# Keeping a bf16 copy of w1 in HBM, written in the first FFN group and reloaded in the other three

## The reference

```python
x = x + attn(_layernorm(x), W_qkv, W_out)
# feed-forward on x of (B, 2048, 1024): w1 (1024, 4096), w2 (4096, 1024)
h = jax.nn.relu(jnp.einsum('bsd,dw->bsw', _layernorm(x), w1) + b1)
x = x + jnp.einsum('bsw,wd->bsd', h, w2) + b2
```

## Time and profile before

| | |
|---|---|
| median of two timed runs | 1320.85 us (1314.60 and 1327.09) |
| the profiled execution, its device time | 1318.62 us |
| its span on the slowest core, core 7 | 1317.1 us |
| spans of the eight cores | 1291.5 to 1317.1 us |
| TensorE busy, core 7 | 989.3 us (75%) |
| VectorE, ScalarE, GpSimd busy | 472.9, 411.4, 101.2 us |
| read from HBM, written to it | 159.54 MB, 8.39 MB |

### The profile page before, as it was taken

The page is one execution under the profiler, slowest core; times in us unless marked ns, Lnnn a source line. Parts: engine busy times, 40 slices in busy tenths (PEclk is TensorE's granted clock), DMA queues, the critical chain, the costliest instruction groups (busy, mean ns, idle before and its releaser), DMA issues.

```text
span 1317.1 us, 12722 instructions; the slowest of 8 cores (1291.5 to 1317.1 us)
## 1 busy us (share of the span) xinstructions
PE 989.3 (75%) x4656; PEld 393.4 (30%) x4656; DVE 472.9 (36%) x638; ACT 411.4 (31%) x443; POOL 101.2 (8%) x131
## 2 busy tenths in 40 slices
PE   0189688585858586776946287997699887987897
PEld 0045222131213132222311133443244333443343
DVE  0451332636354544536351632313240324122301
ACT  0044076574757566564758100001000100010000
POOL 2200200000000000000000001110102001200110
PEclk9999878696979788897968588999999888998899
DMA  9900711010000002000200069896779768988876
GB/s 245 137 4 1 72 16 10 1 17 0 9 9 0 1 0 33 0 1 1 33 0 1 0 93 126 130 163 128 109 130 152 157 93 131 151 166 127 126 119 141
DMA packets 94332, 93.19 MB, mean 71 GB/s; under 512 B 40000, under 2 KB 72768, under 8 KB 94272
## 3 DMA queue, kind: packets, MB, share of 16 engines
q0 software_dynamic: 85248, 75.57, 41.2%
q1 hardware_dynamic: 9024, 16.80, 4.1%
HBM read 159.54 MB, written 8.39 MB: 127 GB/s over the span
## 4 chain that ended last, share of the span: by engine, by line
PE 63%; DVE 14%; DMA 13%; issue 4%; ACT 3%; DVEq 2%; ACTq 0%; POOL 0%; POOLq 0%
PE arena L720 17%; PE arena L675 13%; PE arena L508 11%; DMA wstage<-w 10%; PE arena L365 9%; PE arena L453 6%; DVE tmp_sb L603 5%; PE arena L287 4%; DVE oscr_sb L525 3%; DVE x_sb L614 3%; DMA wstage<-wout 2%; DVEq L51 2%; PE arena L468 2%; PE arena L239 1%; DMA x_sb<-x 1%
## 5 line engine op out<-in xcount | busy, mean ns | idle before, releaser
L481 ACT ACTIVATE p_sb<-arena,cst_sb 128x1024 bf16<-128x1024 f32 (+1 forms) x320 | 290.9, 986 | 100.3 <-PE arena L453 61.4
L508 PE MATMUL arena<-p_sb,vaug_h 128*128 128x512 bf16 (+3 forms) x640 | 192.2, 386 | 144.7 <-DVE oscr_sb L525 94.3
L675 PE MATMUL arena<-lnf_sb,wstage 128*128 128x512 bf16 x1024 | 250.1, 410 | 60.4 <-DMA wstage<-w 54.6
L720 PE MATMUL arena<-w2stage,h_sb 128*128 128x512 bf16 x1024 | 221.7, 379 | 4.0 <-DVE h_sb L688 4.0
L688 DVE TENSOR_SCALAR h_sb<-arena,b1c_sb 128x512 bf16<-128x512 f32 x128 | 96.1, 751 | 224.1 <-PE arena L675 224.1
L675 PEld LDWEIGHTS arena<-lnf_sb,wstage 128*128 128x128 bf16 x1024 | 105.4, 104 | 204.0 <-issue 102.4
L720 PEld LDWEIGHTS arena<-w2stage,h_sb 128*128 128x128 bf16 x1024 | 99.9, 98 | 125.8 <-issue 5.9
L365 PE MATMUL arena<-lnf_sb,wstage 128*128 128x512 bf16 x512 | 125.6, 402 | 8.3 <-DMA wstage<-wqkv 8.3
L453 PE MATMUL arena<-qpair,kpair 64*128 64x512 bf16 (+3 forms) x640 | 125.1, 387 | 4.9 <-DVE kpair L388 4.9
L508 PEld LDWEIGHTS arena<-p_sb,vaug_h 128*128 128x128 bf16 x640 | 42.7, 100 | 207.3 <-issue 206.0
L381 DVE CAST qpair<-arena 64x512 bf16<-64x512 f32 x64 | 43.7, 683 | 150.1 <-PE arena L365 149.5
(11 more groups left out here) (37 smaller groups left out, 495.1 us busy)
## 6 DMA issues: line engine op xcount, KB each, us to landing
wstage<-w POOLq DMA_DIRECT2D x32, 1024.0 KB, 11.1
w2stage<-w POOLq DMA_DIRECT2D x64, 512.0 KB, 6.9
x_sb<-x SPq DMA_DIRECT2D x4, 2048.0 KB, 25.7
y<-y_sb SPq DMA_DIRECT2D x16, 512.0 KB, 5.1
wstage<-wqkv POOLq DMA_DIRECT2D x24, 256.0 KB, 12.7
wstage<-wout POOLq DMA_DIRECT2D x4, 512.0 KB, 21.1
b1c_sb<-b SPq DMA_DIRECT2D x32, 0.5 KB, 7.2
identb_sb<-identf POOLq DMA_DIRECT2D x1, 32.0 KB, 8.6
```

The source lines that it names most:

```text
L481: e.activation(AP(p_sb, (si_ % 3) * 1024, [[3 * 1024, 128], [512, 2], [1, w_]]), AP(arena, b_ + off_, [[AR, 128], [512, 2], [1, w_]]), AF. ...
L508: e.matmul(AP(arena, (4 + hx) * 512 + off_, [[AR, 128], [1, w_]]), vaug_h[:, hx, j_ * 128:(j_ + 1) * 128], AP(p_sb, (si_ % 3) * 1024 + hx ...
L675: (lambda s_, dc_, fb_, wp_: lambda e: e.matmul(bankap(fb_, TF), AP(wstage, s_ * 1024 + dc_ * 512 + wp_ * 128, [[8 * 1024, 128], [1, 128]] ...
L720: (lambda s_, ww_, c2_, dh_, t_: lambda e: e.matmul(bankap(t_, 512), h1_sb[:, ww_, 128 * c2_:128 * (c2_ + 1)], w2stage[:, s_, 512 * dh_:51 ...
```

## The change

A DRAM tensor w1b of 1024 x 4096 bf16 is added (8 MB for each core). In group 0 the quads of w1 are loaded and cast by POOL as before, and ScalarE also stores each quad from wstage to w1b. The slots of such a quad are free when its last matmul and its store are both done. In groups 1 to 3 the quads are loaded from w1b in bf16, by DMAs that ScalarE issues. w2 is loaded as before. The other edits let `slot_free` hold a list, and add the new semaphores to the final wait.

```diff
+    w1b_d = nc.dram_tensor("w1b", [D, W1N], BF16, kind="Internal")
...
-        def load_slot_quad(in_ap, out_dims):
+        def _slot_waits(s, n):
+            w = []
+            for i in range(n):
+                v = slot_free[s + i]
+                w.extend(v if isinstance(v, list) else [v])
+            return w
+
+        def load_slot_quad(in_ap, out_dims, eng="gpsimd", pre="dw"):
...
-            w = [slot_free[s + i] for i in range(4)]
-            cnt = add("gpsimd",
+            cnt = add(eng,
                       (lambda oa, ia: lambda e: e.dma_start(oa, ia))(out_ap, in_ap),
-                      waits=w, inc=f"dw{s}", amt=16)
-            return s, (f"dw{s}", cnt)
+                      waits=_slot_waits(s, 4), inc=f"{pre}{s}", amt=16)
+            return s, (f"{pre}{s}", cnt)
...
                 if ww % 4 == 0:
-                    sp, dwp = load_slot_quad(
-                        AP(w1_d, 128 * ww,
-                           [[W1N, 128], [128 * W1N, DC], [1, 512]]),
-                        [[512, DC], [1, 512]])
+                    w1ap = [[W1N, 128], [128 * W1N, DC], [1, 512]]
+                    if g == 0:
+                        sp, dwp = load_slot_quad(
+                            AP(w1_d, 128 * ww, w1ap),
+                            [[512, DC], [1, 512]])
+                        dsb_c = add("scalar",
+                                    (lambda s_, ww_, a_: lambda e:
+                                     e.dma_start(
+                                         AP(w1b_d, 128 * ww_, a_),
+                                         AP(wstage, s_ * 1024,
+                                            [[8 * 1024, 128], [512, DC],
+                                             [1, 512]])))(sp, ww, w1ap),
+                                    waits=[dwp],
+                                    inc=f"dsb{(ww // 4) % 2}", amt=16)
+                        wb_pend = (f"dsb{(ww // 4) % 2}", dsb_c)
+                    else:
+                        sp, dwp = load_slot_quad(
+                            AP(w1b_d, 128 * ww, w1ap),
+                            [[512, DC], [1, 512]],
+                            eng="scalar", pre="dh")
+                        wb_pend = None
...
                     for i in range(4):
-                        slot_free[s + i] = ("mm", mm_f1)
+                        slot_free[s + i] = ([("mm", mm_f1), wb_pend]
+                                            if wb_pend else ("mm", mm_f1))
```

More of the change, by code:

```diff
@@ L40, in build_program @@
     y_d = nc.dram_tensor("y", [S, D], F32, kind="ExternalOutput")
+    w1b_d = nc.dram_tensor("w1b", [D, W1N], BF16, kind="Internal")
     seq = []
-    C = {"dx": 0, "dwb": 0, "dbc": 0, "dy0": 0, "dy1": 0, "dy2": 0, "dy3": 0,
+    C = {"dx": 0, "dwb": 0, "dbc": 0, "dsb0": 0, "dsb1": 0,
[1 row of a table added]
          "dq0": 0, "dq1": 0, "dq2": 0, "dq3": 0,
@@ L48, in build_program @@
         C[f"dw{_i}"] = 0
+        C[f"dh{_i}"] = 0
     def vdrain():
@@ L132, in load_slot @@
                       (lambda oa, ia: lambda e: e.dma_start(oa, ia))(out_ap, in_ap),
-                      waits=[slot_free[s]], inc=f"dw{s}", amt=16)
+                      waits=_slot_waits(s, 1), inc=f"dw{s}", amt=16)
             return s, (f"dw{s}", cnt)
-        def load_slot_quad(in_ap, out_dims):
+        def _slot_waits(s, n):
[5 more added lines that the diff above has]
+        def load_slot_quad(in_ap, out_dims, eng="gpsimd", pre="dw"):
             while slot_ctr[0] % 4:
@@ L153, in load_slot_pair @@
             out_ap = AP(wstage, s * 1024, [[8 * 1024, 128]] + out_dims)
-            w = [slot_free[s], slot_free[s + 1]]
+            w = _slot_waits(s, 2)
             cnt = add("gpsimd",
@@ L776, in build_program @@
                 f1_bank_free[b] = out_bank_free[b]
-        add("sync", None, waits=[("dx", C["dx"]), ("dbc", C["dbc"])] +
+        add("sync", None, waits=[("dx", C["dx"]), ("dbc", C["dbc"]),
+                                 ("dsb0", C["dsb0"]), ("dsb1", C["dsb1"])] +
                           [(f"dy{i}", C[f"dy{i}"]) for i in range(4)] +
-                          [(f"dq{i}", C[f"dq{i}"]) for i in range(4)])
+                          [(f"dq{i}", C[f"dq{i}"]) for i in range(4)] +
+                          [(f"dh{i}", C[f"dh{i}"]) for i in range(8)])
         add("gpsimd", None,
```

## The result

The changed kernel took 1302.61 us in the median of 11 runs, the kernel before 1319.61 us in 10. The ratio is 0.988, with an interval of 0.985 to 0.991: 16 us or 1.2% faster. A second measurement, beside the last experiment, gave 0.986 (0.981 to 0.990). The forecast was 1294.3 us, 1.8% faster.

What follows compares the result with a forecast made beforehand. The prediction took w1 loading to bound the first half of each feed-forward group. From 1318.6 us it took 32.3 for groups 1 to 3 and added 8 for group 0's stores, giving 1294.3 us, range 1272 to 1322.

Steps and rivals of the forecast that it cites:

- The bound and its threshold: w1 half of each group: w1 loading limits; a load landing within 6.98 us of issue is hidden, above that excess is paid.
- The cost of a bf16 load: Groups 1 to 3: 4.1 us of engine work, 1.5 fixed and 0.9 of issuing, so landing in 6.5 us.
- the line through the two casting loads: DMA packet cost from casting w1 and w2 loads: 47 ns per KB read over 17 ns, so 64 ns per 1 KB.
- The exposed first load: Start of groups 1 to 3: the first load, behind ScalarE's copies, loses its cover and is exposed for 6.5 us.
- The stores in group 0: Group 0's w1 half: eight 1 MB stores, 3.5 us of work each, lose 8 us, between 0 and 28.
- the hold, my second way to the same sum: Group 0: a slot waits for its store before reloading; its chain takes 22 to 23 us per pair of quads.
- The row of the mixed window: Trace window where y stores and w1 loads together filled a DMA share of 0.90; taken to mean stores aren't free.
- The w2 halves: Second half of each group: stays at 55.41 us, with moved traffic counted at nothing.
- The first (1273 us): Rival for the whole kernel: loads land in about 4 us, stores run beside loads; 1273 us, chance 0.20.
- The second: Rival in groups 1 to 3: loads land in 7.8 us, a wait replaces the one removed; 1316 us, chance 0.16.
- The third: Rival for loads and stores: a packet of 1 KB written costs 111 ns whatever is read; 1373 us, chance 0.10.
- the 2% line: Whole kernel: a measurement can tell about 2% (26 us) from no change, a line at 1294.4 us.

Runs made afterwards that it cites:

- the last experiment: precopy_w2 and, beside it on the same chip, the changed kernel measured again; ratios to the kernel before 0.942 and 0.986.
- bf16_pool: The changed kernel, but POOL issues the bf16 loads of groups 1 to 3, where it issued the casting ones; ratio to the kernel before 0.966.
- y_late: The changed kernel, but SyncE sends the y stores of groups 0 to 2 behind the next group's first two loads; ratio 0.977, 1290.15 us.
- stores_only: The changed kernel, but groups 1 to 3 load float32 w1 by casting POOL loads as before, so w1b is written and never read; ratio 1.009.
- stores_no_hold: stores_only, but stores of the same shape come from lnf_sb and the slots don't wait for them; ratio 1.004.
- early: The changed kernel, but ScalarE issues the first two quads of groups 1 to 3 ahead of its four copies; ratio 0.968, 1283.39 us.
- split_queues: The changed kernel, but in groups 1 to 3 POOL issues the first two bf16 quads and ScalarE the other six; ratio 0.966.
- precopy_w2: precopy_paced, but group 0's first four w2 loads wait for attention's last instruction, not the first quad's matmuls; ratio 0.942, 1250.35 us.
- precopy_paced: split_queues without quad stores; POOL's HBM-to-HBM casting copies write w1b in attention, each held until TensorE reaches its head pair; ratio 0.952, 1257.30 us.

## Why the prediction was right or wrong

**The bound and its threshold: right.** The w1 half waited for its loads. Once a load landed inside a quad's 6.98 us, the waits inside a group went, and with them the matmuls at 1.2 GHz behind them: 256 matmuls in 57 to 58 us in place of 64 in 14 to 17.

**The cost of a bf16 load: right to 0.6 us, with its fixed part split wrongly.** A stretch of group 1 in the changed kernel, 935 to 975 us, gives it:

```profile
q10 hardware_dynamic: 5709, 5.75, 50.5%
...
wstage<-w1b ACTq DMA_DIRECT2D x5, 1024.0 KB, 6.0
```

50.5% of 40 us over 5709 packets are 57 ns each, 3.6 us a load; the line through the two casting loads gave 64 ns and 4.1 us. (On cores 1 and 7 the same stretch gives 51 ns.) The landing of 5.9 us was forecast as 6.5, so 2.3 us are left beside the work, where the sum had 1.5 fixed and 0.9 of issuing. The total is right and the split isn't: I had allowed 2.4 us for ScalarE to issue a load of 1024 rows, and an issue holds its queue for 0.37 us. The Trainium skill ("DMA: Bandwidth & Descriptors", section "Anatomy of one DMA") has, for a DMA on the software queue, about 2 us plus the bytes at 436 GB/s, an estimate of 4.4 us here. This case's loads are slower on either queue, 5.9 us on ScalarE's and 6.7 on POOL's in bf16_pool, and the rate is part of it: 1.05 MB in 3.4 to 3.6 us is 290 to 310 GB/s.

**The exposed first load: right in kind, 4 us too small in each group.** The step that failed is the sentence that the y stores and the early w2 loads "are nearly through by then". The first load was costed as if alone, 6.5 us after the last copy. It waited 12.0 us on the mean after the last transpose, 10.7 after the copy. The w2 loads were nearly through indeed: on core 0, whose first load left at 910.51 us, 0.05 MB of them moved between 910 and 925 us, though POOL sent the last at 903.58. The y stores weren't: 1.90 of their 2.10 MB moved in that stretch. They leave 2 to 6 us before the load and are 5.2 us of work (1.3 us each). y_late takes them away and finds 7.3 us, or 6.0 after the copy, about the forecast size. I counted a transfer that had been issued as one that was done.

The groups' account closes in the table's measure. The first waits cost 3 x 4.2 = 12.6 us more than forecast. The 3 us a group for a slow start and late loads were 1.2 too many, 3.6 in all. And the forecast started from core 7, whose groups 1 to 3 are 4.5 us longer in sum than the mean core's. Together that is 13.5 us, close to the 12.9 between the 32.3 us forecast for these groups and the 19.4 of the table.

**The stores in group 0: right.** 8 us were forecast for group 0, 8.9 came, and stores_only alone gave 8.3. A store is 3.2 us of work where I took 3.5. Traffic is most of it by the profile of stores_no_hold; the hold, my second way to the same sum, is the smaller part there, and the measured times leave its size open. The row of the mixed window spoke rightly for a price.

**The w2 halves: right for the change,** 55.41 us. early shows how little was needed to lose that.

**The rivals.** The first (1273 us) needed a load in 4 us; it took 5.9. The second had the right kind of event, a wait in the place of the one removed, at another place: not in each pair, but once at a group's start. The third, one price for a packet of any size, is refuted by 57 ns against 111 ns.

The time lay inside the range, and the gain is clear of noise but below the 2% line, on which the forecast sat. Some luck is in the time: the groups gained 13 us less than forecast, and part of that came back because the slowest core drew nearer to the others, which the sum didn't have. Of the wait at each group's start, the place in ScalarE's list is the cause (early and bf16_pool both remove it), and the y stores are somewhat under half of its size (4.7 of 10.7 us).

## What to carry to other kernels

When a load moves to another engine's queue, look at what stands ahead of it there and what it was prefetched behind before: here 24 loads landed in about half the time, and more than half of the gain (70.7 us a group in place of the 60 to 61 of early and bf16_pool, from 77.2) was lost on the three that lost their prefetch. A queue of its own is good for the load that is needed next, and bad for one that is needed later: such a load belongs behind the urgent ones on the same queue. Data that is only cast and reused can be cast while the DMA engines idle, in another phase of the kernel; that was worth more than the change itself (from 0.966 in split_queues to 0.942 in precopy_w2).

## What the runs showed of the hardware that was not expected

- An issue of a load of 1024 rows held ScalarE's queue for 0.37 us, less than the 0.98 us of a y store of 128 rows on SyncE, so the number of rows alone doesn't set the time of an issue. The two are on different engines, and no run issues one DMA from both. The view of the line that issues the loads in the changed kernel gives the smallest, the median and the largest duration in ns:

```profile
L153 ACTq DMA_DIRECT2D wstage<-w1b x24: 366/366/788, 910.5 to 1231.6; - x24
```

- Two queues share the engines even when one has far more time: in early, w1b loads took 25 us to land, and w2 loads 13.8. The Trainium skill ("DMA: Bandwidth & Descriptors", section "Queues, rings and completion order") says each engine goes round robin between the queue rows with work, by packets; the 846 and 1079 packets of the two queues in that stretch agree in kind, where the shares are 71.7% and 30.1%.
- A copy from HBM to HBM with a cast, eight times 1 MB written, ran beside attention without changing its length in precopy_paced and precopy_w2 (starts of 747.0 and 748.2 us, 747.4 before).
- The granted clock between 150 and 300 us was 0.75 on cores 0 and 1 of the changed kernel's profile and 0.91 on core 3, with the same instructions. The feed-forward part of these two starts 8 to 16 us later than on the other six; no run here tells the cause.
